# The descriptor space of dynamic DMAs: 2048 bytes of a partition instead of 8192, in a kernel that issues 6707 gathers from GpSimd

## The reference

```python
idx = jnp.clip(yf, 0, H - 1).astype(jnp.int32) * W + jnp.clip(xf, 0, W - 1).astype(jnp.int32)
v = jax.vmap(lambda im, i: im[i])(img, idx)          # a gather by computed indices
...
samp = bilinear_sample(img, iy, ix, Hin, Win)
return jnp.einsum('nghwpc,nhwgp->nhwgc', samp, mask_sm).reshape(N, H, W, C)
```

## Time and profile before

| | before |
|---|---|
| median of 2 runs | 8979.07 us (8978.62 to 8979.51) |
| span of the profiled execution | 14670.7 us |
| gathers at L1328 | 6707 |
| busy: TensorE, VectorE, ScalarE, GpSimd | 7831.1, 6704.9, 6815.4, 6413.8 us |

### The profile page before, as it was taken

The page is one execution under the profiler, slowest core; times in us unless marked ns, Lnnn a source line. Parts: engine busy times, 40 slices in busy tenths (PEclk is TensorE's granted clock), DMA queues, the critical chain, the costliest instruction groups (busy, mean ns, idle before and its releaser), DMA issues.

```text
span 14670.7 us, 162317 instructions
## 1 busy us (share of the span) xinstructions
PE 7831.1 (53%) x48435; PEld 3785.6 (26%) x48435; DVE 6704.9 (46%) x19495; ACT 6815.4 (46%) x8248; POOL 6413.8 (44%) x6711
## 2 busy tenths in 40 slices
PE   4445655455555555555554555555555455444567
PEld 2122222222222222222222222222222222222234
DVE  4444434444444444444444444454444444344333
ACT  0234634455444554445444454444544355443465
POOL 4544444444444444444444444444444444444430
PEclk6667767777777777777777777777777777776778
DMA  2111111111111111111111111111111111222325
GB/s 64 41 50 39 36 38 39 46 41 38 37 41 49 36 40 38 42 49 34 40 37 46 45 34 39 38 48 44 37 39 35 51 40 37 55 62 63 107 58 162
DMA packets 559311, 703.51 MB, mean 48 GB/s; under 512 B 256976, under 2 KB 371536, under 8 KB 556288
## 3 DMA queue, kind: packets, MB, share of 16 engines
q0 software_dynamic: 214624, 439.98, 11.0%
q1 hardware_dynamic: 343808, 252.97, 6.1%
HBM read 579.54 MB, written 112.84 MB: 47 GB/s over the span
## 4 chain that ended last, share of the span: by engine, by line
another core or an unknown queue 37%; ACT 17%; DVE 16%; issue 13%; PE 12%; DVEq 5%; DMA 1%; SPq 0%; ACTq 0%
ACT tanh L1882 14%; PE score_ps L2072 5%; DVEq L1347 5%; DVE pool_mem L1564 2%; PE side_ps L2012 1%; DVE y L1573 1%; PE value_ps L2101 1%; PE side_ps L1982 1%; DVE expoT L1641 1%; ACT L1892 1%; DVE pool_mem L1551 1%; PE turn_ps L1951 1%; ACT L1867 1%; ACT expo L1892 1%
## 5 line engine op out<-in xcount | busy, mean ns | idle before, releaser
L1882 ACT ACTIVATE tanh<-key_rep,query 128x896 f32<-128x896 f32 (+7 forms) x6400 | 5565.3, 951 | 4618.0 <-remote 2987.3
L1328 POOL DMA_INDIRECT pool_mem<-patches_odd,pool_mem x3375 | 3226.1, 956 | 4002.7 <-DVE y L1573 2977.5
L1328 POOL DMA_INDIRECT pool_mem<-patches_even,pool_mem x3332 | 3187.6, 957 | 3857.4 <-DVE y L1573 2815.5
L2072 PE MATMUL score_ps<-tanh,score_w 128*32 128x512 f32 (+3 forms) x24320 | 3461.1, 604 | 1933.9 <-ACT tanh L1882 1057.1
L2072 PEld LDWEIGHTS score_ps<-tanh,score_w 128*32 128x32 f32 x24320 | 826.2, 120 | 3979.9 <-issue 2624.8
L2101 PE MATMUL value_ps<-values,expoT 128*128 128x129 f32 (+1 forms) x5200 | 908.4, 317 | 408.3 <-issue 329.7
L1564 DVE TENSOR_TENSOR pool_mem<-pool_mem 128x384 f32<-128x384 f32 (+1 forms) x2352 | 1089.1, 532 | 12.9 <-issue 7.6
L1573 DVE TENSOR_REDUCE y<-pool_mem 128x64 f32<-128x2304 f32 x392 | 999.1, 2549 | 31.9 <-issue 9.6
L2012 PE MATMUL side_ps<-near_map,hatT 112*64 112x480 f32 x2792 | 806.3, 685 | 318.6 <-DVEq L1347 206.0
L2101 PEld LDWEIGHTS value_ps<-values,expoT 128*128 128x128 f32 (+1 forms) x5200 | 790.6, 223 | 524.8 <-issue 399.8
L1892 ACT ACTIVATE expo<-score_ps,tiny 128x896 f32<-128x896 f32 (+9 forms) x416 | 383.4, 922 | 1017.1 <-remote 743.1
(11 more groups left out here) (194 smaller groups left out, 8060.3 us busy)
## 6 DMA issues: line engine op xcount, KB each, us to landing
pool_mem<-in_weight SPq DMA_DIRECT2D x64, 1024.0 KB, 9.3
pool_mem<-patches_odd,pool_mem POOLq DMA_INDIRECT x3375
pool_mem<-patches_even,pool_mem POOLq DMA_INDIRECT x3332
patches_even<-pool_mem SPq DMA_DIRECT2D x104, 256.0 KB, 2.0
patches_odd<-pool_mem SPq DMA_DIRECT2D x104, 256.0 KB
pool_mem<-in_x SPq DMA_DIRECT2D x56, 224.0 KB
x_tok<-in_x SPq DMA_DIRECT2D x192, 64.0 KB
x_d<-x SPq DMA_DIRECT2D x192, 64.0 KB
```

The lines of the kernel that those rows point to most:

```text
L1328: pool.indirect_dma_start(gathered[:, b, j * 4 * CG:(j + 1) * 4 * CG], None, patches_flat[int(odd)], bass.IndirectOffsetOnAxis(ap=index[:, ...
L1882: nc.scalar.activation(tanh[:, TANH_AT[ui][0]:TANH_AT[ui][1]], key_rep[:, lo:lo + w], ACT.Tanh, bias=query[:, col:col + 1]).then_inc(tanh_ ...
L2072: last = mm(score_ps[32 * col:32 * col + 32, ci % 2, lo:hi], score_w[:, place], tanh[:, TANH_AT[ui][0] + lo:TANH_AT[ui][0] + hi], start=pl ...
```

## The change

One number in the construction of the program: the reserved space is 2048 bytes of each partition in place of 8192. No instruction, wait, tensor or order of steps is edited.

```diff
-    nc = bacc.Bacc("TRN2", target_bir_lowering=False, num_devices=1, dynamic_dma_scratch_size=8192)
+    nc = bacc.Bacc("TRN2", target_bir_lowering=False, num_devices=1, dynamic_dma_scratch_size=2048)
```

## The result

The changed kernel takes 9808.01 us (9801.52 to 9814.5, 2 runs) against 8979.07 us: the ratio is 1.0923 [1.0906, 1.0941]. It is 829 us slower, where no difference was forecast and 9063 us was the upper end.

What follows compares the result with a forecast made beforehand. GpSimd's gather issue was taken to bound the run. Gathers under way, turns of the space and place of tensors were each taken at 0, so 8979 + 0 = 8979 us, range 8937 to 9063 us.

Steps and rivals of the forecast that it cites:

- The bound: GpSimd's gather issue at L1328, 6707 x 1.25 us, 8854 us with both ends, bounds a run of 8979.07 us.
- Gathers under way: Descriptor space at L1328: one or two gathers outstanding, six at worst; room for seven costs 0, for two 40 us.
- How often the space is gone through: Reuse of descriptor space at L1328, four times as often: taken at 0, 84 us for the range, bound 252 us.
- Place of the tensors: Tensors behind the space may move by 6144 bytes per partition: taken at 0, at best 42 us less.
- Rival (1): Turns of the space cost GpSimd time at L1328: up to 252 us, 9231 us; chance 0.07.
- Rival (2): The new space holds only one or two gathers: 10,700 us more at one, 40 us at two; chance 0.03.
- Rival (3): SP's transfers, the `near_map` loads at L1157, use the space too: 257 us more, 9236 us; chance 0.03.
- Rival (4): The number doesn't reach these descriptors, or the space never held anything: 8979 us, no row changed; chance 0.06.
- rival (5): A better place of the tensors shortens gathers at L1328: 8937 us, 42 us less; chance 0.03.
- The last sentence of the prediction: Prediction is wrong if descriptor writing waits for all earlier ones at the space's end, such waits formerly lost among 84 us.
- The size of a gather: By the skill's 16-byte descriptors, nine per engine, 2048 bytes hold 14 gathers against 56 before; cost still 0.

Runs made afterwards that it cites:

- second profile of before: The kernel before, unchanged, run and profiled again for a recording that had not slowed it: 8983.76 us, ratio 1.0001.
- A3: Theory formed after the runs with two semaphores in turn: a full space waits for its oldest gather that is last on its semaphore, then releases everything up to it.

## Why the prediction was wrong

**The bound.** Right: GpSimd's issue of gathers bounds the run. In the second profile of before the gathers go from 72.0 to 8621.6 us, 1.275 us each where 1.25 was taken, with 360 us behind the last. So the idle time is paid almost one for one, as the table shows. What was wrong is a side remark: that recording slows this kernel. Only the execution of the earlier trace rows was longer than a run; thirteen others, one of them of the same kernel, were recorded at the length of a run. What made that one long is not known.

**Gathers under way.** This is the step that failed: "If the new one holds seven or more the cost is 0." The new space does hold more than seven: the first gap stands behind 14 gathers. But the number under way, one or two and six at the worst, is not what fills the space. At gather 15 it was full, though the oldest gather in it had landed some 15 us before. By A3 they are released by semaphore: until the last gather on a semaphore has landed, all on it stay. A sub-tile puts 17 on one semaphore, the new space holds 14, and so once per sub-tile it is full of gathers with one common semaphore, whose last was issued just before. That one takes 2.16 us to land, and GpSimd goes on 1.0 us later; 3.16 us less its own 0.94 us are the 2.22 us of the first gap. The condition of little loss is that the space holds one whole group of gathers on a semaphore and two more, so that three spacings of 1.25 us pass before the group must be gone: with none more (2560 bytes, 17) the loss was whole, with one more (2752 bytes, the last image) 57.8 us in 42 gaps, with two more (the other images there) 11.3 us, and with 11 more (4096 bytes) nothing. The old space, 56 gathers, met it without showing it, which is why had no mark.

**How often the space is gone through.** The bounds were taken from the old space, where each passage finds an earlier sub-tile complete. That the earlier trace rows show no mark was true and did not carry over: the price is not paid per passage but depends on which gather must be waited for. The 252 us as a bound failed with it.

**Place of the tensors.** Taken at 0, and nothing speaks against it: with 4096 bytes whatever lies behind the space can move too, and the ratio is 1.0; in the changed kernel's own 2048 bytes, with two semaphores, it is 1.0014.

**The rivals.** Rival (1) had the side and the place, a gap at L1328 at a distance that is not that of the images; its price was a third of the measured 829 us, since it was bounded by the excess of gathers that never had to wait. Rival (2) would have made the spacing long everywhere or in jams, with no more than two gathers in the space; here 14 pass before the first gap. Rival (3) would have lengthened SP's issue at L1157, where the medians are 1512 ns after and 1564 ns in the second profile of before. Rival (4) is excluded by the first gap, and rival (5) by the time, with a mean gather of 968 ns against 970 in the second profile of before. The last sentence of the prediction came near ("waits for all earlier ones at the end of the space") and was not given a price. It could have had one from the prediction's own numbers: a wait for the former gather at 1.6 us, once in 14 gathers by its estimate from the Trainium skill, is 479 x 1.6 = 766 us. By rows alone, with 1.75 gathers or more in the new space, no such price could be told.

**The size of a gather.** The first gap ahead of gather 8, 15 and 18 with 1024, 2048 and 2560 bytes puts a gather between 2560 / 18 = 142.2 and 1024 / 7 = 146.3 bytes of the space. By "DMA: Bandwidth & Descriptors" of the Trainium skill a descriptor has 16 bytes (Terms), and one transfer of 1 MiB to 128 partitions takes 9 write descriptors on each engine (The descriptor swizzle). An estimate from these figures, taken over to a gather of 64 KB, is 144 bytes; the runs agree with it. That the sum would stay the same by this figure was my conclusion and not the Trainium skill's. The rule of the Trainium skill in "Debugging Trainium Hangs", Descriptor Overflow, did not show: all kernels ended, down to 1024 bytes, and GpSimd waited instead.

## What to carry to other kernels

As far as these runs go, space for descriptors should hold the longest row of DMAs that GpSimd issues on one semaphore, plus those that follow while the last one lands (two here, at 1.25 us each); count DMAs per semaphore before cutting it, not DMAs under way. Where the space is wanted for data, change the semaphore inside the row (after nine of 17 here): 2048 bytes then cost 13 us in place of 829, and with blocks of four even 1024 bytes cost 76 us. A resource that shows no wait at its old size gives no bound for its price at a smaller one.

## What the runs showed of the hardware

GpSimd's writing of descriptors can wait without any wait in the program, and the profile shows it only as idle time "issue" ahead of the next indirect DMA: 2.16 us per sub-tile in the changed kernel, with the end 1.0 us after the landing of the gather waited for, at the median of its gaps. What it waits for follows the semaphores that the DMAs raise: with the same 14 gathers in the space it was the last gather with one semaphore, the last but one with two in turn, and with three in turn hardly any wait was left (38.8 us in all). A3 is the rule that fits all thirteen kernels; it is inferred from the places and lengths of the gaps, and how GpSimd keeps its books was not seen. Nor was it tried why going on takes 1.0 us after a landing.
